# Placing every edge of the first order with TensorE instead of scattering half of them to DRAM

## The reference

```python
def _gnn_layer(x, row, col, W, b, g, beta):
    neigh = x[col]
    agg = jax.ops.segment_sum(neigh, row, num_segments=n)
    ...
x = x + _L0_gnn_ref(_layernorm(x), stack([src, dst]), ...)   # two such layers: sum by src, gather by dst
...
x = x + _L1_gnn_ref(_layernorm(x), src, dst, edge_weight, ...)  # sum by dst, gather by src, weighted
```

## Time and profile before

| What | us |
|---|---|
| median of 3 executions (7270.54 to 7273.53) | 7271.44 |
| span of the profiled execution | 7265.6 |
| stage sort, start to its last instruction | 0 to 990.6 |
| of this, the scatters to table0 issued by GpSimd | 82.4 to 605.3 |
| of this, the placing loop | 721.6 to 988.8 |
| stage sum0, first gather | 997.5 |
| TensorE busy, of the whole span | 3646.1 (50%) |
| VectorE busy | 2657.8 (37%) |
| GpSimd busy | 3769.2 (52%) |

### The profile page before, as it was taken

The page is one execution under the profiler, slowest core; times in us unless marked ns, Lnnn a source line. Parts: engine busy times, 40 slices in busy tenths (PEclk is TensorE's granted clock), DMA queues, the critical chain, the costliest instruction groups (busy, mean ns, idle before and its releaser), DMA issues. The chain is left out here.

```text
span 7265.6 us, 61921 instructions
## 1 busy us (share of the span) xinstructions
PE 3646.1 (50%) x13991; PEld 2632.2 (36%) x13992; DVE 2657.8 (37%) x6350; ACT 899.9 (12%) x2400; POOL 3769.2 (52%) x3797
## 2 busy tenths in 40 slices
PE   4112974444544445444431222299992455555729
PEld 1001543333333333333221000178881334333517
DVE  5115864444433444444340000011114455555661
ACT  0000950000003000000230000022221100000322
POOL 4772036666663666666537777700005566666321
PEclk7556987777777777777665555599996678787859
DMA  3000113333321333332011000022214233333250
GB/s 136 1 0 30 21 49 92 92 92 92 91 61 61 90 92 91 92 92 83 21 58 59 4 2 8 4 75 81 83 57 137 88 90 91 90 91 91 70 162 18
DMA packets 290147, 497.59 MB, mean 68 GB/s; under 512 B 99253, under 2 KB 182880, under 8 KB 290048
## 3 DMA queue, kind: packets, MB, share of 16 engines
q0 software_dynamic: 163264, 345.19, 16.7%
q1 hardware_dynamic: 125696, 150.28, 6.3%
q10 hardware_dynamic: 1088, 1.05, 0.1%
HBM read 487.50 MB, written 92.89 MB: 80 GB/s over the span
## 5 line engine op out<-in xcount | busy, mean ns | idle before, releaser
L970 PE MATMUL sum_sums<-sum_got,sum_onehot 128*128 x4992 | 1613.7, 484 | 1690.7 <-DVE acc L1132 1360.6
L902 POOL DMA_INDIRECT sum_got<-xn,edge_row x1568 | 1541.5, 983 | 1138.9 <-issue 451.4
L970 PEld LDWEIGHTS sum_sums<-sum_got,sum_onehot 128*128 128x128 f32 x4992 | 1166.3, 244 | 2121.9 <-issue 1915.4
L1132 DVE TENSOR_TENSOR acc<-acc,sum_sums 128x257 f32 (+1 forms) x2496 | 1052.7, 422 | 1777.8 <-remote 1241.3
L902 POOL DMA_INDIRECT sum_got<-h,edge_row x784 | 754.4, 962 | 453.3 <-issue 228.4
L1270 POOL DMA_INDIRECT table<-rec,addr x784 | 802.8, 1024 | 298.5 <-issue 277.4
L1866 PE MATMUL moe_f_ps_y<-xb,moe_f_hT 128*128 128x256 f32 x1792 | 478.8, 399 | 317.3 <-issue 317.2
L1850 PE MATMUL moe_f_ps_h<-moe_f_xT,xb 128*128 128x256 f32 x1792 | 473.1, 396 | 303.9 <-issue 303.9
L1931 DVE TENSOR_TENSOR moe_f_y<-moe_f_ps_y,moe_b 128x256 f32<-128x256 f32 x112 | 42.4, 420 | 1362.4 <-DMA table<-acc 718.5
L1698 POOL DMA_INDIRECT moe_out_c_got<-moe_out,place_i x98 | 95.0, 970 | 824.5 <-PEq L1656 785.1
L1270 POOL DMA_INDIRECT table<-sort_rec,sort_addr x392 | 400.0, 1020 | 201.8 <-issue 122.9
(11 more groups left out here) (460 smaller groups left out, 3297.0 us busy)
## 6 DMA issues: line engine op xcount, KB each, us to landing
xb<-in_L_ffn_W SPq DMA_DIRECT2D x112, 1024.0 KB
sum_got<-xn,edge_row POOLq DMA_INDIRECT x1568
moe_in<-acc SPq DMA_DIRECT2D x28, 512.0 KB
moe_f_xin<-moe_in SPq DMA_DIRECT2D x56, 256.0 KB
moe_out<-moe_f_y SPq DMA_DIRECT2D x56, 256.0 KB
xn<-xb SPq DMA_DIRECT2D x14, 896.0 KB
table<-rec,addr POOLq DMA_INDIRECT x784
sum_got<-h,edge_row POOLq DMA_INDIRECT x784
```

The source lines that it names most:

```text
L902: pool.indirect_dma_start(got[:, c % SU, 0:D], None, source, bass.IndirectOffsetOnAxis(ap=p.edge_row[:, c:c + 1], axis=0)).then_inc(s_got[ ...
L970: mm = nc.tensor.matmul(sums[k % 2][j], onehot[:, (k % QUARTERS) * HALF + j, :], flat(got[:, bass.ds(where[n % PLAN], 1), :]), start=True, ...
L1132: v.tensor_tensor(a, a, sums[k % 2][j], ALU.add).then_inc(s_added[j], 1)
```

## The change: table0 goes, and the placing loop takes all 784 columns

`SENT` and `PLACED` are gone. rank(0) and rank(1) stay as they are, one after the other; `places` and the six small instructions run once behind both, over 784 columns. The placing loop runs over 784 columns on VectorE, ScalarE and TensorE. table0, its fill, GpSimd's 392 scatters, their waits, the load in sum0 and one addition there are gone. For table1 nothing changes. `addr0` makes room for `spread`, of the same size. Cut to its core:

```diff
-SENT = 392
-PLACED = EC - SENT
...
-        edge_col, edge_lane = (p.edge_weight[:, k * PLACED:(k + 1) * PLACED] for k in range(2))
-        edge_high, edge_low = (p.edge_row[:, k * PLACED:(k + 1) * PLACED].bitcast(F32) for k in range(2))
+        edge_col, edge_lane = p.edge_row[:].bitcast(F32), p.edge_weight[:, 0:EC]
+        edge_high, edge_low = spread, rec[0].bitcast(F32)
...
-            pool.wait_ge(s_prefill, 32)
-            pool.wait_ge(s_addr, 1)
-            scatter.run(pool, 0, SENT)
...
-            with act.Fori(0, PLACED // U) as i:
+            with act.Fori(0, EC // U) as i:
...
-            sp.dma_start(dram["table0"].rearrange("(p q) a -> p (q a)", p=P), fill[:, 0:QW]).then_inc(s_prefill, 16)
...
+            sp.wait_ge(s_prefill, 16)
...
-            with pe.Fori(0, PLACED // U) as i:
+            with pe.Fori(0, EC // U) as i:
...
             rank(0)
-            part = slice(0, SENT)
-            places(part)
-            address(0, part)
             rank(1)
-            part = slice(SENT, EC)
-            places(part)
-            c.done(nc.vector.tensor_copy(edge_lane, lane[:, part]))
...
+            places(slice(0, EC))
+            c.done(nc.vector.tensor_copy(edge_lane, lane[:]))
...
-            with dve.Fori(0, PLACED // U) as i:
+            with dve.Fori(0, EC // U) as i:
...
-def sum_over_edges(p, source, order, weighted, table, own=None, centre=()):
+def sum_over_edges(p, source, order, weighted, fresh, table, own=None, centre=()):
...
-            if table is not None:
-                sp.dma_start(raw, table.rearrange("(p q) a -> p q a", p=P)).then_inc(s_raw, 16)
+            if fresh:
+                if weighted:
+                    sp.dma_start(raw, table.rearrange("(p q) a -> p q a", p=P)).then_inc(s_raw, 16)
...
-                dve.wait_ge(s_raw, 16)
-                whole = p.edge_local[:, 0:CH]
-                if not weighted:
-
-                    c.link(v.tensor_tensor(whole, whole, raw[:, :, 0], ALU.add))
-                    c.link(v.tensor_copy(raw[:, :, 0], whole))
+                if weighted:
+                    dve.wait_ge(s_raw, 16)
+                else:
+                    c.link(v.tensor_scalar(raw[:, :, 0], p.edge_local[:, 0:CH], float(NONE << KEYBITS), None, ALU.add))
```

More of the change, by code:

```diff
@@ L71 @@
 assert CH % SU == 0 and CH * P >= E and BLOCKS * BLOCK == CH and BLOCK < P and CH < 1 << 10
-assert PLACED == MID and PLACED % U == 0
+assert EC % U == 0
 assert STEPS * U == NT and MOE_TILES % 2 == 0
@@ L184, in sort_edges_and_normalize @@
         s_const, s_keys0, s_keys1, s_keyfill = s("s_const"), s("s_keys0"), s("s_keys1"), s("s_keyfill")
-        s_dve, s_addr, s_fill, s_prefill = s("s_dve"), s("s_addr"), s("s_fill"), s("s_prefill")
+        s_dve, s_fill, s_prefill = s("s_dve"), s("s_fill"), s("s_prefill")
         s_zero, s_xpad, s_x, s_xnout = s("s_zero"), s("s_xpad"), s("s_x"), s("s_xnout")
-        scatter = Scatter(p, ctx, dram["table0"], addr[0], rec[0].unsqueeze(2))
         s_wload, s_wT, s_wcopied = s("s_wload"), s("s_wT"), s("s_wcopied")
@@ L201, in sort_edges_and_normalize @@
         pair = [t[:, :, 0:MID] for t in (placed[0], placed[1], counted)]
-        runs = [(0, 0, SENT, bank, (0, 1, 2, 0, 1, 2, 3)), (0, SENT, EC, bank, (0, 1, 2, 0, 1, 2, 3)),
+        runs = [(0, 0, MID, bank, (0, 1, 2, 0, 1, 2, 3)), (0, MID, EC, bank, (0, 1, 2, 0, 1, 2, 3)),
                 (1, 0, EC, pair, (0, 1, 2, 0, 1, 2, 1))]
@@ L445, in places @@
                 c.link(nc.vector.tensor_single_scalar(win_i[:, part], pos_i[:, part], 7, ALU.arith_shift_right))
-            def address(k, part):
-                nc.vector.scalar_tensor_tensor(out=addr[k][:, part], in0=lane[:, part], scalar=float(QW),
-                                               in1=win_i[:, part], op0=ALU.mult, op1=ALU.add).then_inc(s_addr, 1)
             def tile_numbers(k):
@@ L494, in _ @@
             rank(0)
-            part = slice(0, SENT)
-            places(part)
-            address(0, part)
             rank(1)
-            part = slice(SENT, EC)
-            places(part)
-            c.done(nc.vector.tensor_copy(edge_lane, lane[:, part]))
[L502 to L505, removed]
+            places(slice(0, EC))
+            c.done(nc.vector.tensor_copy(edge_lane, lane[:]))
+            c.done(nc.vector.tensor_copy(edge_col, win_i[:]))
+            c.link(nc.vector.tensor_single_scalar(pos_i[:], rec[0], LOWBITS, ALU.arith_shift_right))
+            c.done(nc.vector.tensor_single_scalar(lane[:], rec[0], LOW - 1, ALU.bitwise_and))
+            c.done(nc.vector.tensor_scalar(edge_high[:], pos_i[:], -float(NONE << (KEYBITS - LOWBITS)), None, ALU.add))
             c.settle()
-            c.link(nc.vector.tensor_copy(edge_low, lane[:, part]))
+            c.link(nc.vector.tensor_copy(edge_low, lane[:]))
             tile_numbers(1)
@@ L513, in _ @@
             places(slice(0, EC))
-            address(1, slice(0, EC))
+            c.link(nc.vector.scalar_tensor_tensor(out=p.addr1[:], in0=lane[:], scalar=float(QW), in1=win_i[:],
+                                                  op0=ALU.mult, op1=ALU.add))
             dve.wait_ge(s_const, 6)
@@ L1110, in _ @@
             v.memset(spare[:, 0:2], 0.0).then_inc(s_added[HALF - 1], 1)
-            if table is None:
+            if not fresh:
                 v.memset(p.acc[:], 0.0).then_inc(s_added[HALF - 1], 1)
@@ L2300, in build @@
     dram = {name: nc.dram_tensor(name, shape, dt).ap() for name, shape, dt in (
-        ("table0", (P * QW, 1), I32), ("table1", (P * QW, 2), I32), ("xn", (NT * P, D), F32),
+        ("table1", (P * QW, 2), I32), ("xn", (NT * P, D), F32),
         ("h1", (NT * P, D), F32), ("x2", (NT * P, D), F32),
@@ L2355, in build @@
         centre += [row_params[name][:] for name in ("L0_gnn_b0", "L0_gnn_b1", "L1_gnn_b_self", "L1_gnn_b_msg")]
-        stage("sum0", sum_over_edges, dram["xn"], 0, False, dram["table0"], None, centre)
+        stage("sum0", sum_over_edges, dram["xn"], 0, False, True, None, None, centre)
         stage("gnn0", gnn_dense, 0, True, row_params["L0_gnn_b0"], row_params["L0_gnn_g0"],
               row_params["L0_gnn_beta0"], ACT.Silu, None, dram["h1"], (0, FEW))
-        stage("sum1", sum_over_edges, dram["h1"], 0, False, None)
+        stage("sum1", sum_over_edges, dram["h1"], 0, False, False, None)
         stage("gnn1", gnn_dense, 1, True, row_params["L0_gnn_b1"], row_params["L0_gnn_g1"],
@@ L2368, in build @@
         stage("moe_out", combine, dram["moe_out"], TOP, p.share, p.norm_out, dram["x2"], dram["xn"])
-        stage("sum2", sum_over_edges, dram["xn"], 1, True, dram["table1"],
+        stage("sum2", sum_over_edges, dram["xn"], 1, True, True, dram["table1"],
               ([p.wT[:, 2, kb, :] for kb in range(KB)], [row_params["L1_gnn_b_self"], row_params["L1_gnn_b_msg"]]))
```

8 lines of the change are left out of this document (4 added, 4 removed).

## The result

| | before | after |
|---|---|---|
| median of 4 runs | 7271.39 us (7270.54 to 7273.53) | 7059.94 us (7057.6 to 7061.14) |
| ratio, 95% interval | | 0.971 (0.9697 to 0.9723) |
| span of the profiled execution | 7265.6 | 7058.6 |

A forecast was written before the change was run, and what follows sets the result against it. From 93 to 631 something tied to scatters in flight was taken to bound the kernel, then TensorE in the placing loop. -470.5 + 259.7 - 1.6 = -212.4 gave 7059 us; range 7040 to 7078 (0.85), 7090 with the lower-clock rival.

The forecast's parts named there:

- rank(1), the small instructions, count(1), rank(2), -470.5: Sort up to rank(2)'s end: without scatters in flight these run at free pace, ending at 215.6 instead of 686.15.
- gets one instruction through: Sort's slow stretch: as if TensorE got one instruction through for every column scattered, 1.44 us each in rank(1).
- The placing loop, +259.7: Placing loop: 392 more columns at 0.663 us each, TensorE binding at full clock, nothing hiding it.
- the rival of the lost clock (7313): Placing loop: TensorE loses the full clock, added columns take 1.31 us instead of 0.663; 7313 us, chance 0.04.
- sum0, -1.6: Start of sum0: no wait for table0 and no addition, so the first gather comes 1.6 us sooner.
- The lower clock in the middle, +24: Sort's middle at TensorE's lower clock: count(1) +14.4, rank(2) +10; 7083 us, chance 0.07.
- The slow pace stays, 7530: rank(1), count(1), rank(2) keep 5 to 11 us a tile, the change only adds +258.4; 7530 us, chance 0.03.
- The rule of the Trainium skill: Objection to the largest term: by it, scatters in flight could cost VectorE a port and TensorE nothing.
- its first term: Sort up to rank(2)'s end: the slow pace ends when the scatters do, a gain of 470.5 us.

The follow-up runs named there:

- e8_kept_again: The changed kernel with the 392 scatters put back, to a table that nothing reads: 7558.58 us, where the kernel before took 7301.23.
- e5_place_half: The changed kernel with the placing loop over 392 of its 784 columns, the other columns' records left out: 5475.28 us, kernel before 5541.01.
- the split at 357 with the loops: The kernel before with 357 columns scattered, 427 placed, TensorE's count and rank as seven-step loops, not 49 unrolled tiles: 5507.51 us (0.9919) and 7252.08 us (0.9976).

## Why the prediction was right, and what it had not seen

| boundary | predicted | after, upper level | after, lower level |
|---|---|---|---|
| rank(1) ends | 117.6 | 117.8 | 118.4 |
| rank(2) ends | 215.6 | 216.0 | 216.6 |
| first product of the placing loop | 251.1 | 252.0 | 252.5 |
| VectorE waits for the last | 776.5 | 777.5 | 778.1 |
| first gather | 785.1 | 785.9 | 786.4 |

*rank(1), the small instructions, count(1), rank(2), -470.5.* Right: rank(2) ends at 216.03, a gain of 470.1. That at the upper level it was the scatters is shown by e8_kept_again, which puts them back and loses 469.2 us again. The prediction said that TensorE "gets one instruction through" per scatter. Read as a picture of instructions that can't start, this doesn't fit: by the record they start on time and are known to be done late, at that pace. That the pace follows the number of scatters, as the sentence has it, was not tested at the upper level; 1.34 to 1.40 us an instruction against 1.28 a scatter is near, not equal.

*The placing loop, +259.7.* Right: from the first product to the wait it takes 525.5 us, against 265.7 in the earlier trace rows, which is +259.8. e5_place_half gives 257.6 for the same columns. The clock was 0.98 in the first 148 us and 1.00 behind them, so the rival of the lost clock (7313) fell.

*sum0, -1.6.* The first gather comes 8.33 us after the wait for the last product, where it took 10.16 before, -1.8. But the rest of the kernel then took 6272.8 us instead of 6268.1, 4.7 more. I had costed it at nothing. Some 4 us of it come from the execution that the earlier trace rows were read from: its span lies 5.8 us under the median, where the executions that are on record with their spans have them 1.7 to 2.0 us under their times. That execution was short itself, and the rest is within the spread of the runs.

*The lower clock in the middle, +24.* It did not come. The clock in rank(2) is 0.87, and count(1) goes as count(0) did.

*The slow pace stays, 7530.* It fell as a forecast, and its price proved sound: with the scatters kept, e8_kept_again takes 7558.58 - 7301.23 = 257.4 us more than the kernel before, where the rival had +258.4.

*The rule of the Trainium skill* (SBUF — State Buffer, "Who interferes with whom": "DMA never contends with a compute engine") agrees with the lower level, where 392 scatters cost 6 us and a flood of single words nothing that can be seen. At the upper level the measurement decides against that sentence as it stands: the same scatters cost 469 us of waiting for TensorE. The page speaks of ports to SBUF, and no run here shows where the two meet.

**What it had not seen** is that its first term depends on the level of the chip. The mechanism was read from one trace and is true of it. That the result was then measured at the level of that trace was luck, since nothing in the prediction reckons with levels: at the lower level the time goes up by 183 us where the forecast took 212 off. The sum there is +257.9 for the placing (the wait for its last product at 778.07 instead of 520.13) - 82.1 (from there to the first gather 8.3 us instead of 90.5) = +175.8, and the change loses 3.3%. Chips 9 and 11 were each met at both levels, chips 1 and 15 at the lower one alone, so it isn't just a matter of which chip one gets. What switches the level was not found; nothing in these kernels did. Of the 1725 us between the levels of the kernel before, the sort has some 387 (first gather at 997.50 against 610.59). Another 780 lie in moe's products: in the changed kernel those of `moe_f_ps_h` last from 3674 to 5274, and from 3269 to 4088 at the lower level.

The one version that was better than the kernel before at both levels is the split at 357 with the loops: 0.9919 at the lower level, 0.9976 at the upper one. Without the loops it was measured at the lower level alone, 0.9918. These gains are clear of the spread of the runs, but small. The changed kernel is better by far at the upper level (0.971) and worse at the lower (1.033).

## What to carry to other kernels

When a stage waits on two things that run beside each other, find out which of them ends last before moving work from one to the other: here the scatters ended 74 us after the placing at one level, and at the other they made everything before the placing wait. A gain that comes from ending interference should be tested by putting the interfering work back with nothing reading it, and on more than one occasion, since the interference may not be there next time. Where both of two paths are busy, shifting a few per cent of the work until they end together was worth 0.8% at the lower level and 0.2% at the upper one, without any bet on the cause.

## What the runs showed of the hardware

- The same kernel on the same chip took 5541 us and later 7301 (chip 9), 5552 and later 7270 (chip 11). Within one measurement the runs agree within 0.4%.
- At the upper level GpSimd's scatters (128 words each, one in 1.28 us) slow down what waits for TensorE to 1.3 to 1.4 us per TensorE instruction; the first 11 us after the first scatter still go at full pace. At the lower level neither is seen. At the upper level gathers (73 in 100 us) leave TensorE 313 instructions in 100 us.
- At the lower level DMA engines 93% busy with single-word copies (49152 packets) leave TensorE and VectorE at their pace: 98 matmuls and 102 VectorE instructions in 38 us, as without them.
- The end of a matmul as the profile models it isn't the moment when others learn of it: 36.65 us lay between them at the end of count(1), beside scatters at the upper level.
